# ScalarE takes the second half of a pending logarithm ahead of the exponentials in each beat

## The reference

```
q, k, v = split(x @ w_qkv.T);  k_y = split_heads(x @ w_ky.T)
L   = einsum(q, k) * scale;    L_y = einsum(q, k_y) * scale
agg = sum(exp(clip(L_y, -15, 15)) * mask, -1) + EPS
r   = log(abs(L) + EPS) - log(agg + EPS)
w   = softplus(r) * mask
A   = w / (sum(w, -1) + EPS)
out = einsum(A, v) @ w_proj.T
x = layernorm(x + out);  x = layernorm(x + ffn(x))
```

## Time and profile before

| | us |
|---|---|
| median of 3 runs | 1345.96 (1344.07 to 1350.18) |
| the profiled execution | 1343.71 |
| its span, first to last instruction | 1342.0 |
| attention, to the start of feed-forward | about 636 |
| of it the loop, 5 trips | 355.5 |

### The profile page before, as it was taken

How to read it: one execution, slowest core, us unless ns; L and a number is a source line. 1 busy time by engine, 2 the same in 40 slices (tenths; PEclk the granted TensorE clock), 3 DMA queues, 4 the chain that set the end, 5 groups by cost and what they waited for, 6 DMA issues and landing times.

```text
span 1342.0 us, 23982 instructions
## 1 busy us (share of the span) xinstructions
PE 1202.2 (90%) x8214; PEld 810.8 (60%) x8214; DVE 733.8 (55%) x1229; ACT 657.3 (49%) x963; POOL 199.2 (15%) x236
## 2 busy tenths in 40 slices
PE   2898898898889889864899999999999999999996
PEld 1444444444444444432688787887877878878785
DVE  2466879796969797774333535326353353443533
ACT  3678878878887888651412323223232241322311
POOL 1423233333333333200000000000000000000000
PEclk8999999999999999987799999999999999999998
DMA  4355656676675846221910000000000000000000
GB/s 139 85 136 133 191 138 208 156 203 158 185 188 163 201 137 157 57 63 48 352 49 16 31 16 32 0 16 31 16 16 16 16 31 16 16 16 16 31 0 17
DMA packets 62667, 117.27 MB, mean 87 GB/s; under 512 B 8992, under 2 KB 14752, under 8 KB 62624
## 3 DMA queue, kind: packets, MB, share of 16 engines
q1 hardware_dynamic: 62624, 116.71, 30.8%
HBM read 46.42 MB, written 19.92 MB: 49 GB/s over the span
## 4 chain that ended last, share of the span: by engine, by line
issue 52%; POOL 0%; DVE 0%; POOLq 0%; DVEq 0%
POOL f_rstd L953 0%; DVE f_res L960 0%; POOLq L1053 0%; DVEq L965 0%; POOL f_minus_half L1051 0%; POOLq L84 0%
## 5 line engine op out<-in xcount | busy, mean ns | idle before, releaser
L1079 ACT ACTIVATE f_h_full<-f_layer_bank,f_scales 128x512 f32<-128x512 f32 x128 | 88.1, 688 | 354.6 <-PE f_layer_bank L1193 354.5
L1193 PE MATMUL f_layer_bank<-f_ha_hi,f_w_all 128*128 128x512 f32 x512 | 204.9, 400 | 2.8 <-DVE f_h_full L1121 2.3
L626 DVE TENSOR_TENSOR w_ring<-score_banks,keep 128x1024 int32<-128x1024 int32 (+1 forms) x192 | 191.5, 1039 | 26.7 <-PE score_banks L790 26.5
L1193 PE MATMUL f_layer_bank<-f_hb_hi,f_w_all 128*128 128x512 f32 x512 | 202.9, 396 | 0.0
L1193 PE MATMUL f_layer_bank<-f_ha_lo,f_w_all 128*128 128x512 f32 x512 | 202.2, 395 | 0.0
L1193 PE MATMUL f_layer_bank<-f_hb_lo,f_w_all 128*128 128x512 f32 x512 | 202.1, 395 | 0.0
L480 ACT ACTIVATE w_ring<-w_ring 128x1024 f32<-128x1024 f32 (+1 forms) x192 | 176.4, 919 | 34.9 <-DVE w_ring L626 34.6
L473 ACT ACTIVATE e_ring<-score_banks 128x1024 f32<-128x1024 f32 (+1 forms) x192 | 158.1, 876 | 35.6 <-PE score_banks L790 35.6
L617 DVE TENSOR_SCALAR e_ring<-e_ring 128x2048 f32<-128x2048 f32 (+1 forms) x96 | 101.0, 1052 | 112.1 <-ACT e_ring L473 112.0
L353 POOL TENSOR_SCALAR_AFFINE_SELECT e_ring<-e_ring 128x512 f32<-128x512 f32 (+1 forms) x96 | 78.5, 818 | 315.4 <-DVE e_ring L617 311.3
L1193 PEld LDWEIGHTS f_layer_bank<-f_ha_hi,f_w_all 128*128 128x128 f32 x512 | 96.2, 188 | 34.4 <-DVE f_ha_lo L1113 6.5
(11 more groups left out here) (116 smaller groups left out, 1794.1 us busy)
## 6 DMA issues: line engine op xcount, KB each, us to landing
piece<-in_wf SPq DMA_DIRECT2D x44, 256.0 KB, 2.8
wf_copy<-piece SPq DMA_DIRECT2D x44, 256.0 KB, 2.9
ky_stack<-ky_hi SPq DMA_DIRECT2D x64, 128.0 KB, 2.6
ky_stack<-ky_lo SPq DMA_DIRECT2D x64, 128.0 KB, 2.7
k_stack<-k_hi SPq DMA_DIRECT2D x64, 128.0 KB, 2.6
k_stack<-k_lo SPq DMA_DIRECT2D x64, 128.0 KB, 2.6
f_w_all<-wf_copy SPq DMA_DIRECT2D x2, 4096.0 KB, 25.7
f_x_turn<-x SPq DMA_DIRECT2D x9, 512.0 KB, 3.3
```

Source lines behind the costliest of these rows:

```text
L626: nc.vector.tensor_tensor(w_ring[:, t % RING, 2 * i:2 * i + 2, 0:cols].bitcast(I32), pair_banks(w_pair(t, i), cols).bitcast(I32), keep[:, ...
L1079: nc.scalar.activation(h_full[m % 2][:], f_bank[m % RING][:], ACT.Gelu, scale=scales[:, 1 + layer, m:m + 1]).then_inc(gelu_done, 1)
L1193: mm = nc.tensor.matmul(out, left.bitcast(dt), right.bitcast(dt), start=first and n == 0, stop=last and n == 1)
```

## The change

In each beat the call of `logs` for the second half of the beat before moves from behind the first group of small copies to the front, ahead of `exps`.

```diff
@@ scalar, slot
                 for t in range(BEATS):
                     sums = sums_of(t, y, w, before)
+                    if sums[1]:
+                        logs(*beat_before(k, t), 1)
                     if y:
                         exps(k, t)
...
                     if t == 5 and y and k.half == 0:
                         v_keep(k)
-                    if sums[1]:
-                        logs(*beat_before(k, t), 1)
                     if t == 0 and 3 in w and k.half == 1:
                         v_sum_keep(k.shift(-1))
```

## The result

The changed kernel takes **1376.83 us** (1376.35 to 1377.40, 4 runs) against 1345.74 us (4 runs) for the kernel before: the ratio is 1.0228, with a 95% interval of 1.0200 to 1.0256. The forecast was 1374 us, range 1358 to 1390. The profiled execution's span went from 1342.0 to 1375.0 us.

What follows compares the result with a forecast made beforehand. Bound by a ring of waits between three nearly full engines. Five trips at 2.3 (half 0) plus 1.5 (half 1) give 19 us, units outside 4.6 + 4.6: +28, from 1346.0 to 1374 us, range 1358 to 1390 (0.80).

Steps and rivals of the forecast that it cites:

- Ring and routes: Loop: waits circle through absolute values, y scores, exponentials, clip; late exponentials and `att_raw` cost five trips 19 us.
- E(1): Exponentials of beat 1, ScalarE, half 0: start about 1.16 us late, behind the second absolute value and a full-size logarithm.
- E(2): Exponentials of beat 2, ScalarE, half 0: 1.16 + 0.96 = 2.12 us late, with one more logarithm ahead.
- W(2): Weight scores of beat 2, TensorE, half 0: wait for that beat's exponentials and move by 2.12 us.
- Y(3): The y scores of beat 3, TensorE, half 0: 1.2 us late, after TensorE's slack takes up part.
- E(4): Exponentials of beat 4, ScalarE, half 0: some 2.35 us late; clip, `att_raw` and the k projection wait for them.
- E(5): Exponentials of beat 5, ScalarE, half 0: 3.3 us late; that beat's logarithm then hides in beat 0's idle time.
- The norm's cover: Half 1, beat 4: norm's statistics on VectorE hide the new logarithm all but 0.02 us; half 1 costs 1.5.
- the clock falls: Rival: TensorE's granted clock in the loop drops from 1.00 to 0.88, adding 43 us, to 1417; chance 0.03.
- Covered: Rival: VectorE's other work and TensorE's queue hide the delays; up to 7 us, 1346 to 1353; chance 0.07.
- faster: Rival: logarithms run inside ScalarE's waits for scores, `sum_weights` stops waiting; at most 6.3 us gained, 1340; chance 0.04.
- all on the path: Rival: each of eight full-size logarithms a trip costs 0.96 us, 7.7 a trip, nothing won back, 1400; chance 0.06.

Runs made afterwards that it cites:

- the runs that open each alone: Changed kernel with second-half logarithm right behind the exponentials, ahead of copies: 73.6 us a trip; changed kernel with half 0's `att_raw` copy ahead of the exponentials: 74.45 us.
- the order above: Second-half logarithm against the kernel before, over 70.7 us a trip: behind the exponentials 2.9, between them in full-size beats 3.4, ahead of them 4.2.
- the pair of runs: Norm's statistics moved from beat 3 to the end of beat 2: on the kernel before 70.7 to 70.15 us a trip, on the changed kernel 74.9 to 74.8.
- The two fastest kernels: Kernel before with norm's statistics in beat 2, 1342.5 us; the same plus beat 1's cast `piece_hi` moved into ScalarE's wait ahead of `ky_full`, 1342.5 us.

## Why the prediction was right, and where it was off

**Ring and routes: right.** The changed kernel lost its time where the prediction put it, in the loop's waits and not in work. That both things that the log delays, the exponentials and `att_raw`, are on the path was claimed from distances in the trace and is now shown by the runs that open each alone. That half-size logarithms are free in beats 0 and 3 is shown by the run that moves only those. The clip turned out to be a third way, worth 0.5 us a trip in the order above.

**Beat by beat, half 0**, from the rows above (plus 59.45) against the steps: E(1) +1.4 where the step had 1.16; `att_raw` +1.4 (1.16); E(2) +2.4 (2.1); W(2) +2.4 (2.1); Y(3) at 319.73, that is 379.18, +1.4 (1.2); E(4) +2.2 (2.35); E(5) +3.0 (3.3). The last two are too small: the trip of the earlier trace rows is the one that was 0.35 longer by a DMA, ahead of its beat 4. Against an undisturbed trip E(4) is +2.5, E(5) +3.3, and half 0 costs 2.55 (2.3).

The surplus of 0.25 arises in beat 0 and comes from the beat 5 before it, whose logarithm the prediction took to hide. Before and after, GpSimd and VectorE at the end of half 1:

```profile
359.84 0.99 POOL L375 TENSOR_TENSOR v_before<-v_before,v_aug 128x128 f32<-128x128 f32 x2
...
360.84 1.21 DVE L674 TENSOR_TENSOR base_v<-base_v,att_raw 128x1024 f32<-128x1024 f32 x1
```

```profile
299.14 0.69 DVE L617 TENSOR_SCALAR e_ring<-e_ring 128x1024 f32<-128x1024 f32 x1 [0.86 <-ACT e_ring L473]
...
300.00 0.68 POOL L353 TENSOR_SCALAR_AFFINE_SELECT e_ring<-e_ring 128x512 f32<-128x512 f32 x1 [2.20 <-DVE e_ring L617]
...
301.01 1.91 POOL L375 TENSOR_TENSOR v_before<-v_before,v_aug 128x128 f32<-128x128 f32 x2
...
301.16 1.45 DVE L674 TENSOR_TENSOR base_v<-base_v,att_raw 128x1024 f32<-128x1024 f32 x1
```

The late E(5) makes the clip late (VectorE idles 0.86 for it where it idled for nothing), the clip makes the mask late, and behind the mask in GpSimd's queue stand the sums of values `v_before`; the values themselves (`v_keep`, done at 299.58) were there in time. On top of that the two additions take 1.91 us instead of 0.99, side by side with a VectorE addition that takes 1.45 instead of 1.21. `sum_values` then waits for `v_before` (0.52 at 302.98; 6.8 us of weight-load waits in the loop in 5 times, none before), and with it TensorE's and ScalarE's small jobs of beat 0, so that L0(0) starts 0.5 us late. The prediction followed beat 5 of a unit only on ScalarE and to W(5).

**Half 1**: 37.2 us a half against 35.6, +1.6 where the step had 1.5. In beat 1 the clip did not move, as forecast: it stands behind `factors` in either kernel. The norm's cover is shown by the trips of the pair of runs.

**The base.** The sum was made on a trip of 71.1, the mean of five. Three of these are at 70.7, one (71.05) had a longer wait for `qc_stack`, and one (72.2) a stretch at half clock. Over the undisturbed trip the change costs 4.2, not 3.8; over the five as they are, 20.0 in all against 19. Half of the error of the per-trip term was hidden by the base. That the forecast's 74.9 us a trip came out to the digit is luck of the same kind: a base 0.4 too long and a cost 0.4 too small. (A small slip: half of the forecast's cost would have put the lower bound at 1360, not 1358.)

**Outside the loop: the units right, the clock missed.** The four units outside were set at 2.3 each. From clip to clip of beat 0 units (1, 0), (1, 1) and (7, 0) cost 2.4, 2.0 and 2.5, so the guess for half 1 was near, though no run says why. To the loop's start it is 4.0 in all, since the changed kernel was 0.5 ahead when unit (1, 0) began; what that half is from stays open (up to the loop the granted clock was 0.93 in the kernel before and 0.99 in this one). Behind the loop it is 6.9 for two units, and another 1.9 where I had 0. There the step on the clock failed ("I count no loss"). The k projection of beat 4 in unit (7, 1), before and after:

```profile
563.11 1.98 PE L747 MATMUL misc_bank<-xv,w_in 128*128 128x512 f32 x4
...
594.47 1.99 PE L884 MATMUL misc_bank<-wp,att_t 128*128 128x256 f32 x8
```

```profile
591.15 3.78 PE L747 MATMUL misc_bank<-xv,w_in 128*128 128x512 f32 x4
...
625.09 3.78 PE L884 MATMUL misc_bank<-wp,att_t 128*128 128x256 f32 x8
```

The same four matmuls take 3.78 us instead of 1.98, and the eight of a `project_out` further on 3.78 instead of 1.99: some 3.6 us of the 33 in two places, about what the last two stretches of the table have over the forecast (6.9 + 1.9 against 4.6). They ran at half clock in one kernel and at full clock in the other. That these 3.6 us are on the path is argued from this match, not shown by a run. The rival "the clock falls" as I priced it, 0.88 throughout the loop, did not come; it came in pieces, mostly where the phase thins out. And what the prediction held against it, that the loop before "holds 1.00", was a rounded mean: from 170 to 173 us the granted clock was 0.54 there.

**Covered, faster, all on the path:** no. The change costs 4.2 us a trip, not the 7.7 of the eight full-size logarithms and not under 1. The wait of `sum_weights` for a logarithm did go away, as the rival "faster" had it, and was worth nothing, since its engine then waited elsewhere.

## What to carry to other kernels

When three engines pass work round a ring and none is full, an instruction on an in-order engine belongs behind the last one that others wait for, in front of a wait that is there anyway; ask of each instruction that it is moved past who waits for that, through small copies that free a bank as well as through the obvious output. An advance is free only where the engine idled at the new place for at least its length. And follow the delay through to the start of the next unit before you say that nobody waits: the last missing quarter of a microsecond here went over VectorE, GpSimd and TensorE back to ScalarE. Before you believe a difference of some us between two whole times, look whether it lies where the change acts.

## What was not expected of the hardware

An addition on GpSimd slowed down beside one on VectorE. In all five turns from half 1 to half 0 in the loop of the changed kernel, and in the run of beats 2 and 5, the two additions of 128x128 to `v_before` take 1.90 to 1.92 us (the longest single one 1.45) where the second overlaps VectorE's addition of 128x1024 to `base_v`, which takes 1.44; in the turns to half 1, where VectorE works on score banks beside them, they take 0.99 to 1.00, and in the kernel before, where VectorE comes to its addition as they end, the two take 0.99 and 1.21. So a delay of 0.6 us at the start of the additions, against the clip of the beat 0 that follows, became 1.5 at their end.

TensorE's clock came down inside a loop whose stage shows 1.00 before and 0.99 after. Four windows of 3 us of the changed kernel, two in an undisturbed trip and the same two a trip later (same columns as above):

```profile
309.10:312.10 3.00, 1.58 (x23) 1.07 (x20) 1.99 (x4) 2.24 (x4) 0.00 (x0) 1.00 0.71 244
312.10:315.10 3.00, 3.00 (x29) 1.41 (x27) 2.50 (x3) 1.75 (x4) 1.46 (x2) 1.00 0.84 257
384.00:387.00 3.00, 1.59 (x23) 1.12 (x20) 2.02 (x3) 2.20 (x4) 0.00 (x0) 1.00 0.73 199
387.00:390.00 3.00, 3.00 (x13) 0.94 (x11) 2.45 (x3) 1.15 (x3) 1.10 (x1) 0.51 0.86 270
```

TensorE had been busy 1.58 and 1.59 us of 3, with the same waits, ahead of both; then it ran at 2.4 GHz once and at 1.2 GHz once, and did 13 matmuls in 3 us instead of 29. That trip took 75.5 us instead of 74.9. The kernel before has such a stretch in one of its five trips, the changed one in two, and the run with the logarithm between the exponentials in four. But five runs have none in the loop, though they wait more than the kernel before: the logarithm right behind the exponentials, ahead in beats 1 and 4 only, between the exponentials at full size, the change with the copy ahead, and the change with the norm's statistics moved. The two fastest kernels have such stretches in two trips each. The Trainium skill ("TensorE: Matmul & The Clock Gate", section "A second HAM failure mode: psum-queue depth-cycling") says that short waits between groups of matmuls can make the clock swing. These rows agree that it happens; that more waiting makes it more frequent does not hold over all these runs, and what decides it stays open.
